# Attention with the PV product in three f32r passes instead of one fp32 pass, two steps behind the scores

## The chip, the cores and the metric

The kernel runs on one core of a Trainium2 chip. The metric is the device time of one execution in microseconds (us). TensorE (PE in the profile) multiplies matrices, VectorE (DVE), ScalarE (ACT) and GpSimd (POOL) work element by element, and SyncE (SP) issues DMAs. Each engine runs its own instructions in order; semaphores tie them together.

## The reference

One adaLN transformer block on x of shape 4 x 512 x 256: layer norm, attention with 16 heads of 128 whose weights are MXFP4 codes times block scales, a second layer norm, and a dense layer with eight routed LoRA experts. All of it is fp32. The change touches one product of the attention:

```python
q = _mxfp4_matmul(x, wq_codes, wq_scales) + bq      # k and v alike
scores = jnp.einsum('bqhd,bkhd->bhqk', q, k) / jnp.sqrt(jnp.float32(HEAD_DIM))
attn = jax.nn.softmax(scores, axis=-1)
out = jnp.einsum('bhqk,bkhd->bqhd', attn, v)        # "PV": 512 x 512 times 512 x 128, per batch and head
...
x = x + ga * attn_out
h = _layernorm(x) * (1 + cb) + sb
x = x + gb * ffn(h)                                  # dense + top-2 LoRA experts
```

## The kernel before

**Tiling.** Heads go two at a time: 8 pairs of heads (`pair(p)`), and in a pair 8 steps s = 0 to 7, one for each of 4 batches and 2 heads, so 64 steps n = 8p + s. Pairs 1 to 6 are a hardware loop (`Fori`), pairs 0 and 7 are written out, with the input transposes in the first and the preparation of the FFN weights in the last. All 512 x 512 scores of a step lie in four PSUM banks, `score_ps[0..3]`, one for each 128 queries.

**Three passes.** `three` (line 875) makes an fp32 product of two f32r matrices and their remainders: hi x hi, hi x lo, lo x hi, three matmuls. Q, K, V projections, scores and the output projection are made so. PV is not: `weighted` (line 934) multiplies fp32 `v` with fp32 transposed probabilities, four matmuls of 128 x 512, each of which the trace shows as two records.

**A step, by engine.** PE: scores of step n in four blocks; projections of q and k for step n+1 (`project`, banks `qv_ps`, `ky_ps`); output projection of the block before last (`out_project`, banks `y_ps` = `score_ps[2:4]`); V projection for n+1 (`project_v`); PV of step n-1 (`weighted`). DVE: four row maxima (`maximum`), reciprocals of the sums (`inverse`), the low parts of o, q and k (`o_low`, `q_low`, `k_low`), four 32 x 32 block transposes of the probabilities (`turn`), and two additions of the projected output to `yT` (`y_add`). ACT: four exponentials, then the high parts `q_high`, `k_high`, then `v_out` and `o_high`. POOL: multiplies the four blocks of probabilities by the reciprocals (line 364), then a share of the preparation of the next pair's weights: `product` (codes times scales) and `parts` (high and low part). SP: 16 DMAs that move the 32 x 32 blocks from `pB` to `pT32`, so that the transposition is whole. ACT also issues the loads of the next pair's weights, three DMAs at the end of each of the steps 0 to 3 (`load_weights`).

**What sets the order.** The order on each engine is that in which the code is written. `turned(par, kt)` is the view of `pT32` that PV reads, 16 runs of 32 numbers; `par` is the parity of the step, for which there are two `pB`, two `pT32` and two banks `o_ps`. `landed` is the semaphore value at which all 16 DMAs of a step have landed.

**The tail.** After the last step PE, DVE, POOL and ACT still make the last PV, two output projections, four batches of second layer norm (`attended`, `statistics`, `ffn_rows`), `ffn_input`, LoRA and dense products.

Of the kernel before, what the change touches and what calls it, by code (L numbers as in the profile page):

```python
# [5 lines left out]
def bass_adaln_mxfp4_attention_moe_lora_kernel(  # L6
# [64 lines left out]
    with ExitStack() as ctx:  # L71
# [26 lines left out]
        v = sb("v", [P, 2, QT, PW])  # L98
# [3 lines left out]
        pT32 = sb("pT32", [P, 2, G, QT, QT, 32])  # L102
        o_hi, o_lo = sb("o_hi", [P, S], f32r), sb("o_lo", [P, S], f32r)
# [58 lines left out]
        o_ps = [bank("o_even"), bank("o_odd")]  # L162
        y_ps = score_ps[2:4]
# [74 lines left out]
        def load_weights(queue, m, p):  # L238
# [57 lines left out]
        def _(pool):  # L296
# [44 lines left out]

            inverse_std(1)
# [16 lines left out]
            def pair(p, first=False, last=False):  # L359
                for s in range(SPP):  # L360
                    n = SPP * p + s
                    for i in range(QT):
                        pool.wait_ge(inv_ok, QT * n + i + 1)
                        pool.tensor_tensor(prob[:, i], prob[:, i], inv_sum[:, i:i + 1].to_broadcast([P, S]),  # L364
                                           ALU.mult).then_inc(prob_ok, 1)
                    if first and s in INPUT_AT:
                        inverse_std(INPUT_AT[s])
                    if s < 2:
                        if s == 0:
                            product("o", p)  # L370
                        if not first:
                            pool.wait_ge(y_mm, DC * (n - 1))
                        parts("o", p, s)
                    elif not last:
                        if s < 5:
                            product("vqk"[s - 2], p + 1)
                        elif s == 6:
                            pool.wait_ge(v_mm, n + 2)
                            parts("v", p + 1, 0)
                        else:  # L380
                            pool.wait_ge(k_mm, n + 2 if s == 5 else n + 1)
                            parts("q", p + 1, s // 6)
                            parts("k", p + 1, s // 6)
# [26 lines left out]
        def _(act):  # L410
# [37 lines left out]
            def v_out(count, par, half):  # L448
                act.wait_ge(v_mm, count)
                act.activation(v[:, par, 2 * half:2 * half + 2, :], qv_ps[:, :].rearrange("p (t f) -> p t f", t=2),  # L450
                               ACT.Copy).then_inc(v_ok, 1)

            def o_high(count, j):
                act.wait_ge(o_mm, count)
                act.activation(o_hi[:, :], o_ps[j][:, :], ACT.Identity, bias=bias_now[:, 2, j:j + 1]).then_inc(o_hi_ok, 1)  # L455
# [16 lines left out]
            def pair(p, first=False, last=False):  # L472
                for s in range(SPP):
# [3 lines left out]
                    if not early:  # L477
                        o_high(n - 1, s % 2)
                    if s == 1:
                        if not early:  # L480
                            act.wait_ge(o_hi_ok, n - 1)
                        act.activation(bias_now[:, 2], bias[:, 2, bass.ds(2 * p, 2)], ACT.Copy).then_inc(bias_ok, 1)
                        act.wait_ge(bias_ok, 2 * p + 2)
# [23 lines left out]
                    if end:  # L507
                        for i in range(2):
                            act.wait_ge(gbb_mm, i + 1)
                            act.activation(gb_row[:, 2 * i:2 * i + 2], (ky_ps, qv_ps)[i][:, :].rearrange("p (b d) -> p b d", b=2),  # L510
                                           ACT.Copy).then_inc(gbb_ok, 1)
                    if not end:
# [5 lines left out]
                    if not end:  # L518
                        v_out(n + 2, batch_of(s + 1) % 2, (s + 1) % 2)
# [57 lines left out]
            ffn_input_out(1)  # L577
            o_high(N, 1)
# [15 lines left out]
        def _(dve):  # L594
# [135 lines left out]
            def pair(p, first=False, last=False):  # L730
                for s in range(SPP):
# [25 lines left out]
                    if new:  # L757
                        dve.wait_ge(ld_x[new], 16)
                    maximum(0)
# [14 lines left out]
                    if not early:  # L774
                        o_low(n - 1, s % 2, head_slice(p, s - 2))
# [8 lines left out]
                    if not end:  # L784
                        q_low(n + 2, head_slice(p, s + 1))
                    turn(2)
                    if new:
                        normalise(new)
                    turn(3)
# [19 lines left out]

            attended(1)  # L810
            o_low(N - 1, 0, slice(FEAT // P - 2, FEAT // P - 1))
# [3 lines left out]
            ffn_rows(1)  # L815
            attended(2)
            o_low(N, 1, slice(FEAT // P - 1, FEAT // P))
            ffn_rows(2)
            for c in range(DC):
                y_add(DC * (N - 1) + c + 1, B - 1, c, False, (o_ps[0], y_ps[0])[c])  # L820
# [53 lines left out]
        def _(pe):  # L874
# [329 lines left out]
```

## Time and profile before

| | us |
|---|---|
| median of 3 runs | 883.76 |
| lowest, highest | 882.42, 885.69 |
| profiled execution | 881.12 |
| its span | 879.0 |
| PE busy in it | 823.7 (94%) |
| DVE, POOL, ACT busy | 617.1, 404.1, 381.8 |
| steps 2 to 63 | about 55 to 798 |

The span is what the instructions cover; 2.1 us lie around it. "Busy" counts instructions only, not waits. In the middle of the run one step takes 11.71 us and a pair 93.7 us. The timeline gives an instruction's start and its duration; one that follows another without a wait starts before the record of the first ends, so the cost of one in a row is the distance of starts.

### The profile page before, as it was taken

How to read it: one execution, taken by the hardware profiler on the slowest of the kernel's cores; microseconds unless marked ns; L12 is line 12 of the kernel's file. 1: busy time of each engine (PE TensorE's matmuls, PEld its weight loads, DVE VectorE, ACT ScalarE, POOL GpSimd, SP SyncE). 2: the span in 40 equal slices, each digit the busy share in tenths (PEclk: the TensorE clock that was granted, in tenths of full speed). 3: DMA queues.
4: the chain of work that ended last, by engine and by line, in shares of the span. 5: the costliest groups of instructions: out<-in, count | busy, mean ns of one | idle time of the engine just before them, and what ended most of it. 6: DMA issues, size and time to landing. Idle time of an engine off the chain costs nothing.

```text
span 879.0 us, 13011 instructions
## 1 busy us (share of the span) xinstructions
PE 823.7 (94%) x3548; PEld 607.9 (69%) x3548; DVE 617.1 (70%) x1268; ACT 381.8 (43%) x852; POOL 404.1 (46%) x439
## 2 busy tenths in 40 slices
PE   3969899999999999999999999999999999998758
PEld 2746677777777777777777777777777777665556
DVE  3767676776777777777767777777777775767563
ACT  2543544444444445544444444544444443442321
POOL 4433355444544555445544554445545552433230
PEclk9999899999999999999999999999999999999889
DMA  6143334443344334443444335533443353333002
GB/s 199 50 111 109 80 83 106 130 123 93 90 131 134 94 89 113 138 118 88 112 132 115 89 89 140 140 88 89 130 133 98 90 154 94 76 84 78 19 1 96
DMA packets 73808, 90.61 MB, mean 103 GB/s; under 512 B 19571, under 2 KB 40501, under 8 KB 73781
## 3 DMA queue, kind: packets, MB, share of 16 engines
q1 hardware_dynamic: 55988, 74.02, 32.9%
q10 hardware_dynamic: 17792, 16.26, 6.2%
q8 instruction: 13, 0.21, 0.1%
q14 instruction: 15, 0.11, 0.0%
HBM read 21.01 MB, written 2.10 MB: 26 GB/s over the span
## 4 chain that ended last, share of the span: by engine, by line
PE 74%; SPq 8%; issue 6%; DVE 5%; POOL 3%; DMA 2%; ACT 2%; POOLq 0%; ACTq 0%; DVEq 0%
PE o_odd L938 12%; PE o_even L938 11%; PE score L878 8%; PE score L880 8%; PE score L879 8%; SPq L281 7%; PE qv L878 5%; PE qv L880 5%; PE qv L879 5%; PE ky L878 3%; PE ky L879 3%; PE ky L880 3%; POOL prob L364 2%; DVE neg_max L741 2%; DMA pT<-pB 1%
## 5 line engine op out<-in xcount | busy, mean ns | idle before, releaser
L364 POOL TENSOR_TENSOR prob<-prob,inv_sum 128x512 f32<-128x512 f32 x256 | 258.5, 1041 | 385.2 <-DVE inv_sum L746 384.9
L741 DVE TENSOR_REDUCE neg_max<-score 128x1 f32<-128x512 f32 x256 | 176.0, 691 | 195.7 <-PE score L880 195.4
L488 ACT ACTIVATE prob<-score,neg_max 128x512 f32<-128x512 f32 x256 | 175.6, 688 | 59.4 <-DVE neg_max L741 59.2
L752 DVE STREAM_TRANSPOSE pB<-prob 128x512 f32<-128x512 f32 x256 | 179.7, 703 | 8.8 <-POOL prob L364 1.0
L878 PE MATMUL score<-k_hi,q_hi 128*128 128x512 f32 x256 | 124.7, 487 | 6.6 <-ACT hT_hi L431 6.4
L938 PE MATMUL o_even<-pT,v 128*128 128x512 f32 x256 | 115.5, 593 | 1.9 <-DMA pT<-pB 1.9
L938 PE MATMUL o_odd<-pT,v 128*128 128x512 f32 x256 | 115.6, 594 | 1.6 <-DMA pT<-pB 1.6
L880 PE MATMUL score<-k_hi,q_lo 128*128 128x512 f32 x256 | 101.4, 396 | 0.0
L879 PE MATMUL score<-k_lo,q_hi 128*128 128x512 f32 x256 | 100.5, 393 | 0.0
L450 ACT ACTIVATE v<-qv 128x512 f32<-128x512 f32 x64 | 38.2, 597 | 134.9 <-PE qv L880 134.9
L701 DVE TENSOR_TENSOR yT<-score,yT 128x512 f32<-128x512 f32 x121 | 77.2, 676 | 3.9 <-PE score L880 3.9
L938 PEld LDWEIGHTS o_odd<-pT,v 128*128 128x128 f32 x256 | 46.2, 190 | 48.6 <-issue 48.0
L938 PEld LDWEIGHTS o_even<-pT,v 128*128 128x128 f32 x256 | 46.2, 190 | 48.4 <-issue 46.4
L878 PE MATMUL qv<-wv_hi,hT_hi 128*128 128x256 f32 x256 | 73.1, 285 | 5.3 <-DVE q_lo L682 5.3
L879 PE MATMUL qv<-wv_lo,hT_hi 128*128 128x256 f32 x256 | 72.9, 285 | 0.0
L880 PE MATMUL qv<-wv_hi,hT_lo 128*128 128x256 f32 x256 | 72.9, 285 | 0.0
L878 PEld LDWEIGHTS score<-k_hi,q_hi 128*128 128x128 f32 x256 | 48.5, 189 | 29.5 <-issue 21.9
L455 ACT ACTIVATE o_hi<-o_even,bias_now 128x512 fp32r<-128x512 f32 x32 | 22.0, 687 | 99.2 <-PE o_even L938 99.2
L879 PEld LDWEIGHTS score<-k_lo,q_hi 128*128 128x128 f32 x256 | 48.7, 190 | 21.5 <-issue 13.2
L446 ACT ACTIVATE k_hi<-ky,bias_now 128x512 fp32r<-128x512 f32 x64 | 44.2, 690 | 42.7 <-PE ky L880 42.7
L455 ACT ACTIVATE o_hi<-o_odd,bias_now 128x512 fp32r<-128x512 f32 x32 | 22.0, 688 | 80.6 <-PE o_odd L938 80.6
L880 PEld LDWEIGHTS score<-k_hi,q_lo 128*128 128x128 f32 x256 | 48.5, 189 | 11.5
(205 smaller groups left out, 1471.6 us busy)
## 6 DMA issues: line engine op xcount, KB each, us to landing
pT<-pB SPq DMA_DIRECT2D x1024, 64.0 KB, 2.0
out_dram<-x_nat SPq DMA_DIRECT2D x8, 256.0 KB, 2.1
stage<-in_L_attn_wv_codes_dram ACTq DMA_DIRECT2D x7, 256.0 KB
stage<-in_L_attn_wv_scales_dram ACTq DMA_DIRECT2D x14, 128.0 KB
stage<-in_L_attn_wq_codes_dram ACTq DMA_DIRECT2D x7, 256.0 KB
stage<-in_L_attn_wq_scales_dram ACTq DMA_DIRECT2D x14, 128.0 KB
stage<-in_L_attn_wk_codes_dram ACTq DMA_DIRECT2D x7, 256.0 KB
stage<-in_L_attn_wk_scales_dram ACTq DMA_DIRECT2D x14, 128.0 KB
```

Source lines behind the costliest of these rows:

```text
L281: sp.dma_start(flat(pT32[32 * g:32 * (g + 1), par, a]), flat(pB[32 * a:32 * (a + 1), par, g])).then_inc(p_land[par], 16)
L364: pool.tensor_tensor(prob[:, i], prob[:, i], inv_sum[:, i:i + 1].to_broadcast([P, S]), ALU.mult).then_inc(prob_ok, 1)
L446: act.activation(k_hi[:, :], ky_ps[:, :], ACT.Identity, bias=bias_now[:, 1, j:j + 1]).then_inc(k_hi_ok, 1)
L455: act.activation(o_hi[:, :], o_ps[j][:, :], ACT.Identity, bias=bias_now[:, 2, j:j + 1]).then_inc(o_hi_ok, 1)
L488: act.activation(prob[:, i], score_ps[i][:, :], ACT.Exp, bias=neg_max[:, i:i + 1], accum_out=row_sum[:, i:i + 1]).then_inc(exp_ok, 1)
L701: dve.tensor_tensor(yT[:, c, tokens(b)], bank[:, :], yT[:, c, tokens(b)], ALU.add).then_inc(y_ok, 1)
L741: dve.tensor_reduce(neg_max[:, i:i + 1], score_ps[i][:, :], AX.X, ALU.max, negate=True).then_inc(max_ok, 1)
L752: dve.transpose(pB[:, s % 2, :, i].rearrange("p g k q -> p k g q"), prob[:, i].rearrange("p (k g q) -> p k g q", k=QT, g=G)).then_inc(pB_o ...
L878: pe.matmul(dst, a_hi, b_hi, start=first, stop=False)
L879: pe.matmul(dst, a_hi, b_lo, start=False, stop=False)
L880: return pe.matmul(dst, a_lo, b_hi, start=False, stop=last)
L938: ins = pe.matmul(o_ps[par][:, :], v[:, vpar, kt, j * HD:(j + 1) * HD], turned(par, kt), start=(kt == 0), stop=(kt == QT - 1))
```

## The change

PV is made with `three`: 12 matmuls of 128 x 512 a step. For that V and the probabilities need high and low parts.

- V: ACT copies the bank twice, to `v_hi` (f32r) and to `v32` (fp32); POOL subtracts (`v_low`). `v_out` moves from the end of a step to the start of the next one, ahead of the exponentials.
- Probabilities: ACT copies the four landed blocks to `pT_hi` (`prob_high`, after `k_high`, ahead of the weight loads); the low parts of blocks 0 and 1 are subtracted on DVE, those of blocks 2 and 3 on POOL (`prob_low`), at the start of their step, ahead of the maxima and of the multiplications.
- PV of step n-2 stands right behind the scores of step n. `o_high` moves behind the exponentials, `o_low` behind the second `turn`.
- One bank `o_ps[0]` takes PV; the other becomes the bank y of output column block 0.
- The high part of the V weights goes from POOL to ACT (step 7), their low part stands on POOL in step 7 behind `v_low`; products and parts of the other weights move by a step or so.
- In the tail, one more PV, with `prob_high` and `prob_low` for the last two steps.

GpSimd:

```diff
+            def v_low(count, par, half):
+                pool.wait_ge(v_hi_ok, count)
+                pool.wait_ge(v_ok, count)
+                pool.tensor_tensor(v_lo[:, par, 2 * half:2 * half + 2], v32[:, :, :],
+                                   v_hi[:, par, 2 * half:2 * half + 2].bitcast(f32), ALU.subtract).then_inc(v_lo_ok, 1)
+
+            def prob_low(n, par):
+                for kt in (2, 3):
+                    pool.wait_ge(p_hi_ok, QT * n + kt + 1)
+                    pool.tensor_tensor(split(pT_lo, kt), turned(par, kt), split(pT_hi, kt).bitcast(f32),
+                                       ALU.subtract).then_inc(p_lo_b, 1)
...
                     n = SPP * p + s
+                    if not (first and s < 2):
+                        prob_low(n - 2, s % 2)
                     for i in range(QT):
...
+                    if not (first and s == 0):
+                        v_low(n + 1, batch_of(s) % 2, s % 2)
...
+                        if s == 3:
+                            product("v", p + 1)
+                            product("q", p + 1)
+                        elif s == 4:
+                            product("k", p + 1)
+                        elif s > 5:
+                            if s == 7:
+                                pool.wait_ge(w_hi_ok["v"], p + 2)
+                                pool.tensor_tensor(w_lo["v"][:, :, :], w32["v"][:, :, :], w_hi["v"][:, :, :].bitcast(f32),
+                                                   ALU.subtract).then_inc(w_ok["v"], 1)
+                            pool.wait_ge(k_mm, n + 1)
+                            parts("q", p + 1, s - 6)
+                            parts("k", p + 1, s - 6)
```

ScalarE:

```diff
+            def prob_high(par, have):
+                act.wait_ge(p_land[par], have)
+                for kt in range(QT):
+                    act.activation(split(pT_hi, kt), turned(par, kt), ACT.Copy).then_inc(p_hi_ok, 1)
...
+                    if not start:
+                        v_out(n + 1, batch_of(s) % 2, s % 2)
...
-                    if not end:
-                        v_out(n + 2, batch_of(s + 1) % 2, (s + 1) % 2)
+                    if not start:
+                        prob_high((s - 1) % 2, landed(p, s - 1))
```

VectorE:

```diff
+            def prob_low(n, par):
+                for kt in (0, 1):
+                    dve.wait_ge(p_hi_ok, QT * n + kt + 1)
+                    dve.tensor_tensor(split(pT_lo, kt), turned(par, kt), split(pT_hi, kt).bitcast(f32),
+                                      ALU.subtract).then_inc(p_lo_a, 1)
...
+                    if not early:
+                        prob_low(n - 2, s % 2)
                     maximum(0)
                     maximum(1)
```

TensorE, `weighted` and the tail:

```diff
-            def weighted(vpar, j, par, have):
-
-                pe.wait_ge(p_land[par], have)
+            def weighted(n, vpar, j):
+
                 for kt in range(QT):
-                    ins = pe.matmul(o_ps[par][:, :], v[:, vpar, kt, j * HD:(j + 1) * HD], turned(par, kt),
-                                    start=(kt == 0), stop=(kt == QT - 1))
+                    pe.wait_ge((p_lo_a, p_lo_b)[kt // 2], 2 * n + kt % 2 + 1)
+                    cut = (slice(None), vpar, kt, slice(j * HD, (j + 1) * HD))
+                    ins = three(o_ps[0][:, :], (v_hi[cut], v_lo[cut]), (pT_hi[:, kt], pT_lo[:, kt]), kt == 0, kt == QT - 1)
...
             ffn_input(1)
+            weighted(N - 1, (B - 1) % 2, 1)
             pe.wait_ge(y_ok, DC * (N - 1))
             rows_of_y(2)
-            weighted((B - 1) % 2, 1, 1, landed(PAIRS - 1, SPP - 1))
```

**VectorE, one step in the last pair.** The names are output<-inputs; `neg_max` is the maxima, `pB` the block transposes, `yT` the additions. Before, from the maxima on:

```order
L741 TENSOR_REDUCE neg_max<-score 128x1 x3
L746 RECIPROCAL inv_sum<-row_sum 128x1
L741 TENSOR_REDUCE neg_max<-score 128x1
L746 RECIPROCAL inv_sum<-row_sum 128x1
L692 SCALAR_TENSOR_TENSOR o_lo<-o_even,vecT,o_hi 128x512
L746 RECIPROCAL inv_sum<-row_sum 128x1
```

And after:

```order
L752 TENSOR_TENSOR yT<-score,yT 128x512
L743 TENSOR_TENSOR pT_lo<-pT,pT_hi 128x512 x2
L792 TENSOR_REDUCE neg_max<-score 128x1 x3
L797 RECIPROCAL inv_sum<-row_sum 128x1
L792 TENSOR_REDUCE neg_max<-score 128x1
L797 RECIPROCAL inv_sum<-row_sum 128x1 x2
L803 STREAM_TRANSPOSE pB<-prob 128x4x4x32
L797 RECIPROCAL inv_sum<-row_sum 128x1
L803 STREAM_TRANSPOSE pB<-prob 128x4x4x32
L737 SCALAR_TENSOR_TENSOR o_lo<-o,vecT,o_hi 128x512
```

Two subtractions with both inputs in SBUF stand between the last addition and the first maximum, and `o_lo` stands two transposes later.

**GpSimd, steps 6 and 7 of a pair** (here of pair 0). `prob` is the multiplication by the reciprocals, `wv`, `wq`, `wk` the weights. Before:

```order
L364 TENSOR_TENSOR prob<-prob,inv_sum 128x512 x4
L332 TENSOR_TENSOR wv_hi<-stage,ones 128x512
L334 TENSOR_TENSOR wv_lo<-stage,wv_hi 128x512
L364 TENSOR_TENSOR prob<-prob,inv_sum 128x512 x4
L332 TENSOR_TENSOR wq_hi<-stage,ones 128x2x128
L334 TENSOR_TENSOR wq_lo<-stage,wq_hi 128x2x128
L332 TENSOR_TENSOR wk_hi<-stage,ones 128x2x128
L334 TENSOR_TENSOR wk_lo<-stage,wk_hi 128x2x128
```

And step 7 after:

```order
L359 TENSOR_TENSOR pT_lo<-pT,pT_hi 128x512 x2
L387 TENSOR_TENSOR prob<-prob,inv_sum 128x512 x4
L353 TENSOR_TENSOR v_lo<-v,v_hi 128x512
L408 TENSOR_TENSOR wv_lo<-stage,wv_hi 128x512
L340 TENSOR_TENSOR wq_hi<-stage,ones 128x2x128
L342 TENSOR_TENSOR wq_lo<-stage,wq_hi 128x2x128
L340 TENSOR_TENSOR wk_hi<-stage,ones 128x2x128
L342 TENSOR_TENSOR wk_lo<-stage,wk_hi 128x2x128
```

Three subtractions are new in every step, and the low part of the V weights has come from step 6 to step 7, the step whose V projection needs it.

## Rows read from the trace of the kernel before

**Rows 1.** The page: span, and busy time of each engine.

```profile
span 879.0 us, 13011 instructions
PE 823.7 (94%) x3548; PEld 607.9 (69%) x3548; DVE 617.1 (70%) x1268; ACT 381.8 (43%) x852; POOL 404.1 (46%) x439
```

**Rows 2.** One pair: stretch, length; busy PE, PEld, DVE, ACT, POOL; PE clock; DMA.

```profile
356.00:450.00 94.00, 94.00 (x402) 68.90 (x401) 69.81 (x139) 44.34 (x101) 47.51 (x50) 1.00 0.43 111
```

**Rows 3.** Chain of work: start, cost on the path, engine, output, line.

```profile
407.78 0.12 PE qv L880
...
408.62 3.44 PE o_odd L938 x8
412.05 0.23 PE score L878
```

**Rows 4.** Timeline, VectorE, one step: start, duration, line, operation [idle before].

```profile
412.78 2.08 DVE L741 TENSOR_REDUCE neg_max<-score 128x1 f32<-128x512 f32 x3 [2.88 <-PE score L880]
414.78 0.15 DVE L746 RECIPROCAL inv_sum<-row_sum 128x1 f32<-128x1 f32 x1
...
417.72 0.71 DVE L682 SCALAR_TENSOR_TENSOR q_lo<-qv,vecT,q_hi 128x512 fp32r<-128x512 f32 x1
418.35 1.44 DVE L752 STREAM_TRANSPOSE pB<-prob 128x512 f32<-128x512 f32 x2
419.72 0.71 DVE L687 SCALAR_TENSOR_TENSOR k_lo<-ky,vecT,k_hi 128x512 fp32r<-128x512 f32 x1
420.35 1.28 DVE L701 TENSOR_TENSOR yT<-score,yT 128x512 f32<-128x512 f32 x2
424.50 2.08 DVE L741 TENSOR_REDUCE neg_max<-score 128x1 f32<-128x512 f32 x3 [2.88 <-PE score L880]
```

**Rows 5.** Timeline, ScalarE, the same step.

```profile
413.51 0.69 ACT L488 ACTIVATE prob<-score,neg_max 128x512 f32<-128x512 f32 x1 [0.67 <-DVE neg_max L741]
...
420.37 0.60 ACT L450 ACTIVATE v<-qv 128x512 f32<-128x512 f32 x1 [2.10 <-PE qv L880]
```

**Rows 6.** Timeline, GpSimd, this step and the one before.

```profile
409.82 1.27 POOL L334 TENSOR_TENSOR wv_lo<-stage,wv_hi 128x512 fp32r<-128x512 f32 x1
415.01 4.03 POOL L364 TENSOR_TENSOR prob<-prob,inv_sum 128x512 f32<-128x512 f32 x4 [3.93 <-DVE inv_sum L746]
...
421.09 0.73 POOL L334 TENSOR_TENSOR wk_lo<-stage,wk_hi 128x256 fp32r<-128x256 f32 x1
```

**Rows 7.** Timeline: VectorE subtractions without and with GpSimd at work.

```profile
16.56 1.29 DVE L640 TENSOR_TENSOR hT_lo<-hT,hT_hi 128x512 fp32r<-128x512 f32 x2
...
38.30 1.70 DVE L640 TENSOR_TENSOR hT_lo<-hT,hT_hi 128x512 fp32r<-128x512 f32 x2
...
38.32 1.12 POOL L332 TENSOR_TENSOR wo_hi<-stage,ones 128x256 fp32r<-128x256 f32 x1
39.52 1.07 POOL L334 TENSOR_TENSOR wo_lo<-stage,wo_hi 128x256 fp32r<-128x256 f32 x1
```

**Rows 8.** SP's waits from 75 to 780 us (total, times, longest), and its DMAs.

```profile
SPq L281 <- DVE pB L752: 100.2, 59, 5.5
...
pT<-pB SPq DMA_DIRECT2D x1024, 64.0 KB, 2.0
```

**Rows 9.** Timeline, ScalarE's queue: the weight loads at a step's end.

```profile
361.78 0.39 ACTq L249 DMA_DIRECT2D stage<-in_L_attn_wk_codes_dram  x1
362.27 1.20 ACTq L253 DMA_DIRECT2D stage<-in_L_attn_wk_scales_dram  x2
```

**Rows 10.** Timeline, PE: the first PV and the scores behind it.

```profile
50.71 3.67 PE L938 MATMUL o_even<-pT,v 128*128 128x512 f32 x8 [1.66 <-DMA pT<-pB]
...
55.01 0.48 PE L878 MATMUL score<-k_hi,q_hi 128*128 128x512 f32 x1
```

**Rows 11.** Timeline, the tail: ScalarE and VectorE.

```profile
824.27 1.44 ACT L554 ACTIVATE pB<-score,modT 128x512 f32<-128x512 f32 x2 [0.33 <-PE score L1093]
825.15 1.29 DVE L720 TENSOR_TENSOR x_nat<-score,x_nat 128x512 f32<-128x512 f32 x2 [1.63 <-PE score L964]
```

More of the change, by code:

```diff
@@ L102, in bass_adaln_mxfp4_attention_moe_lora_kernel @@
         pT32 = sb("pT32", [P, 2, G, QT, QT, 32])
+        pT_hi = sb("pT_hi", [P, QT, S], f32r)
+        pT_lo = sb("pT_lo", [P, QT, S], f32r)
         o_hi, o_lo = sb("o_hi", [P, S], f32r), sb("o_lo", [P, S], f32r)
@@ L391, in _ @@
             N = SPP * PAIRS
+            prob_low(N - 2, 0)
             gate(2)
@@ L394, in _ @@
             inverse_std(B + 1)
+            prob_low(N - 1, 1)
             times_gb(0)
@@ L476, in pair @@
                     early = first and s < 2
[L477 to L483, printed above, removed]
+                    if not start:
+                        v_out(n + 1, batch_of(s) % 2, s % 2)
+                    if s == SPP - 1 and not last:
+                        act.wait_ge(w_prod["v"], p + 2)
+                        act.activation(w_hi["v"][:, :, :], w32["v"][:, :, :], ACT.Copy).then_inc(w_hi_ok["v"], 1)
                     for i in range(QT):
@@ L577, in _ @@
             ffn_input_out(1)
+            prob_high(1, landed(PAIRS - 1, SPP - 1))
             o_high(N, 1)
@@ L783, in pair @@
                     turn(1)
-                    if not end:
-                        q_low(n + 2, head_slice(p, s + 1))
+                    if not early:
+                        o_low(n - 1, head_slice(p, s - 2))
                     turn(2)
@@ L788, in pair @@
                         normalise(new)
+                    if not end:
+                        q_low(n + 2, head_slice(p, s + 1))
                     turn(3)
@@ L808, in _ @@
             N = SPP * PAIRS
+            prob_low(N - 2, 0)
             attended(1)
-            o_low(N - 1, 0, slice(FEAT // P - 2, FEAT // P - 1))
+            o_low(N - 1, slice(FEAT // P - 2, FEAT // P - 1))
             ffn_rows(0)
@@ L1009, in pair @@
                             pe.wait_ge(exp_ok, QT * (n - 1) + i + 1)
-                        if i >= 2 and not (first and s < 3):
-                            pe.wait_ge(y_ok, DC * (n - 3) + i - 1)
+                        if i == 3 and not (first and s < 3):
+                            pe.wait_ge(y_ok, DC * (n - 2))
                         if i >= 2 and first and s - 1 in INPUT_AT:
@@ L1016, in pair @@
                               True, True).then_inc(s_mm, 1)
+                    if not early:
+                        pe.wait_ge(v_lo_ok, n - s % 2)
+                        if first and s == 2:
+                            pe.wait_ge(h_hi, DC * 2)
+                        if not (first and s < 3):
+                            pe.wait_ge(o_ok, n - 2)
+                        if end:
+                            pe.wait_ge(gbb_ok, 2)
+                        weighted(n - 2, batch_of(s - 2) % 2, s % 2)
                     if end:
-                        pe.wait_ge(gbb_ok, 2)
+                        pe.wait_ge(v_ok, n + 1)
                         rows_of_y(0)
@@ L1050, in pair @@
                         project_v(batch_of(nxt), nxt % 2).then_inc(v_mm, 1)
-                    if not start:
-                        pe.wait_ge(v_ok, n + s % 2)
-                        if first and s == 1:
-                            pe.wait_ge(h_hi, DC * 2)
-                        if not (first and s < 3):
-                            pe.wait_ge(o_ok, n - 2)
-                        weighted(batch_of(s - 1) % 2, (s - 1) % 2, (s - 1) % 2, landed(p, s - 1))
                     if first and s in INPUT_AT:
```

77 lines of the change are left out of this document (42 added, 35 removed).

## The prediction

> **What bounds the kernel now.** The page first [rows 1]: PE is busy 823.7 of 879.0 us, DVE 617.1, POOL 404.1, ACT 381.8. A pair in the middle [rows 2]: PE is busy all of its 94 us at full clock (1.00, the 2.4 GHz level), DVE 69.8, POOL 47.5, ACT 44.3. So in the loop PE sets the time, and a step is what its matmuls cost on the path [rows 3]: 0.227 us for 512 columns in one f32r pass, 0.12 for 256, 3.44 for PV. 12 (scores) + 12 (q, k) + 6 (output) passes are 6.81, twelve half ones (V) 1.43, PV 3.44: 11.68. DVE's first maxima are 11.72 apart [rows 4], which agrees.
>
> **PE: what is removed.** 12 passes x 0.227 = 2.73 replace 3.44: 0.71 less, so 11.0 us a step, 88 a pair for 93.7. Over 61 steps that is 43 us, if PE stays the bound.
>
> **The next bounds.** *SP.* It waits 100.2 us in 705 [rows 8], so 16 issues take (705 - 100) / 60 steps = 10.05 us, and a transfer lands 2.0 us after its issue. A block turned at X is in `pT32` at X + 12.2. Throughput holds (10.05 < 11.0), latency is long.
>
> *DVE.* From the first maximum to the end of the second addition it takes 8.8 us (412.78 to 421.6) [rows 4]. `o_low` no longer fills the time until the first product comes from POOL (0.23 after the reciprocal starts, then 1.04 [rows 4, 6]), which adds 0.6. So 9.4: three maxima 2.0, from there to the fourth transpose's end 5.5, `k_low` and additions 1.9. To this comes D, the time of the two subtractions. Free of others two cost 0.60 each (1.29 recorded for two [rows 7]): D = 1.2, step 10.6, hidden under PE's 11.0.
>
> *POOL.* A subtraction of two 128x512 SBUF inputs costs 1.27, the four multiplications 4.03, the four parts of a q/k slice 2.75 [rows 6]. New per step are two subtractions (2.54) and `v_low` (1.27): 4.03 + 3.81 = 7.85 without weights, 10.6 in step 6, 11.9 in step 7, about 77.5 us a pair.
>
> *ACT.* New: four copies of landed blocks. No row shows a copy from SBUF in such runs; V's copy from PSUM is 0.60 long, and exponentials, 0.69 long with their read, stand 0.69 apart [rows 5]. I take 0.55 each, between 0.5 and 0.7. The second copy of V adds 0.5. In steps 0 to 3 the loads' three DMA issues (0.39 + 1.20, with gaps 1.7 [rows 9]) now stand between `prob_high` and the next step's `v_out`, thus ahead of the exponentials. They were hidden by an idle ACT. The ring over two steps is X + 12.2 (landing) + 2.2 (copies) + 1.0 (V) + 0.8 (exponential) + 5.5 (to the next X of that parity) = 21.7, 10.85 a step; with the loads 23.4, 11.7 a step. So even undisturbed, four of eight steps get little of the 0.71.
>
> **Where the gain goes: two engines at one port.** [Rows 7] is what decides. Two DVE subtractions with both inputs in SBUF took 1.29 while POOL stood still, and 1.70 while it worked; POOL's two operations in that place took 1.12 and 1.07, for 0.61 and 0.72 otherwise. They excluded each other: DVE's first ran, POOL's began behind it (0.5 late), DVE's second behind POOL's (0.4 late). In the loop before no DVE operation has two SBUF inputs; the change puts two into every step, and every POOL operation there reads SBUF.
>
> *By the rule of the Trainium skill* ("SBUF — State Buffer", Who interferes with whom) a DVE operation with two SBUF inputs and a GpSimd operation that reads SBUF exclude each other for the whole instruction. The trace agrees (0.4 and 0.5 us). Without that rule the sum would be the rival "no collision" below.
>
> When do they meet? Take DVE's last addition as zero and T as the step. The previous X is at -1.9, the one that counts at -1.9 - T; landing is at 10.3 - T, and POOL's first `prob_low` (third copy done, +1.75) can start at 12.05 - T. With T = 11.0 that is 1.05, after DVE's second subtraction started (0.6): no meeting. With T of 11.5 or more it is before 0.6: then POOL's 1.27 goes between DVE's two, D = 0.6 + 1.27 + 0.6 = 2.5, and T = 9.4 + 2.5 = 11.9, which keeps them meeting. If POOL comes first as well, D is 3.7 and T 13.1. T is pushed over 11.5 by the loads on ACT (11.7), by the two products of step 3, which end 0.4 us after DVE wants the port, and by steps 6 and 7. I take T = 11.9, D's lower value: at 12.05 - 11.9 = 0.15 DVE is just first.
>
> **A pair.** Step 7: POOL's multiplications start 2.0 + 0.23 behind D, about 5.9 us after PE's scores; + 4.03 + 1.3 (`v_low`) + 1.3 (low part of the V weights) = 12.5, when PE's V projection may start; it wanted to at 10.5. So about 14.2. The stall lets DVE catch up: steps 0 and 1 about 11.0 and 11.2. Steps 2 to 6 take 11.9, and 0.7 more once, for step 3's second product. Sum 11.0 + 11.2 + 59.5 + 0.7 + 14.2 = 96.6, for 93.7: +2.9.
>
> **The ends.** Start: step 1 loses its PV; scores that began at 55.01 can begin when the inputs are transposed, about 51.7: -3.3 [rows 10]. Tail: PV of block 63 now needs `prob_high`, which stands on ACT behind `ffn_input_out(1)` (ends 825.7 [rows 11]), then POOL's two subtractions. With 2.0 us of lag from DVE's longer sequence: 827.7 + 1.75 + 2.54 + last block 0.7 + row transposes 0.9 = 833.7, for 825.15 when `attended(2)` starts now [rows 11]. PE made those rows ahead of PV before and makes them behind it after. What follows is a chain of DVE and POOL: +8.6.
>
> **The sum** against the profiled 881.1: start -3.3; pair 0 from step 3: +3.5; six pairs x 2.9 = +17.4; pair 7, seven steps without weight work: 0 (11.0 + 11.2 + 59.5 = 81.7 for 82.0); tail +8.6. 881.1 + 26.2 = 907.3. The median before stands 0.3% over the profiled time; I say 908.
>
> **Rivals.**
> *No collision, PE bound (faster).* If DVE's second subtraction goes ahead of a waiting POOL, D stays near 1.2 and T is the larger of 11.0 and the ring, whose slack in steps 5 to 8 pays some of the loads. Pair: 88 + 2 (loads) + 1.5 (V weights, step 7) = 91.5, -2.2 each. 881 - 3.3 - 7.5 x 2.2 + 8.6 = 870; without the loads' cost 860. It holds as long as POOL's first `prob_low` comes later than 0.6 after DVE's first. For it: in light steps that is so. Against it: [rows 7], and steps 3, 6, 7, where POOL is still at work. If PE were the bound in every step and the tail free: 840, which needs every cover to hold.
>
> *The gain is just eaten.* T about 11.5 between the two regimes, a pair 93.5: 881 - 3.3 + 8.6 = 886, or 881 if the tail's lag is half.
>
> *Worse.* POOL first at the port often (D 3.1 on average, T 12.5), or POOL slower on runs of 32 numbers, which no row shows: +3 a pair more, 930. PE's clock could fall to 1.2 GHz behind the stall of step 7; each such time costs up to 2 us: 920.
>
> *The change doesn't do what it says.* The order above shows the 12 passes in one row behind the scores, so that PV itself is shorter I take as given.
>
> **How the numbers follow.** Collision kept up (895 to 922): 0.52; worse (over 922): 0.12; gain just eaten (878 to 895): 0.16; no collision (under 878): 0.20. The range takes the first, the third and most of the fourth, from 866 to 924: about 0.8. Faster by over 0.5% (under 879.3): 0.21; within 0.5%, about what a measurement of this kernel can tell from no change: 0.08; slower: 0.71.
>
> **What would show it.** Right: PV on PE 2.73 us long; PE no longer all busy in the loop, waiting for `p_lo`, `o_lo` or `q_lo`; steps of 11.9 and one of 14 a pair; DVE's `pT_lo` subtractions with a mean near 1.2 us instead of 0.69, and POOL's `pT_lo` over 1.3; `attended(2)` some 8 us later after the last scores than now. Wrong: DVE's subtractions at 0.69, steps of 11.0 to 11.4 and PE busy all the time. A mean of POOL's `pT_lo` far over 1.3 without DVE at work would be the worse case. If the steps after 0 to 3 alone are long and ACT never waits there, the loads are the cause and not the port.

## The result, and the profile of the changed kernel

The changed kernel takes 911.03 us (median of 4 runs, 906.94 to 915.88), the kernel before 883.09: ratio 1.033 with a 95% interval of 1.030 to 1.036. The profiled execution took 906.94 us, its span is 905.0. Forecast was 908.

The page of the changed kernel, to be held against [rows 1]:

```profile
span 905.0 us, 14369 instructions
PE 808.7 (89%) x3804; PEld 651.5 (72%) x3804; DVE 773.5 (85%) x1396; ACT 545.4 (60%) x1179; POOL 672.1 (74%) x624
```

PE is busy 15 us less and waits more. DVE is busy 156 us more, POOL 268, ACT 164. One pair in the loop (columns as in [rows 2]):

```profile
434.50:530.70 96.20, 92.02 (x433) 73.45 (x432) 89.69 (x153) 64.50 (x141) 81.28 (x74) 1.00 0.42 109
```

PE, busy all the time in [rows 2], now stands idle 4.2 us of each pair at full clock; DVE is busy 89.7 of 96.2 us, for 69.8 of 94. Where the 26 us of the span come from, read from the first maxima of the steps on DVE:

| stretch | before | changed | difference |
|---|---|---|---|
| start, from the span's start to step 8 | 141.0 | 148.9 | +7.9 |
| six pairs of the loop | 565.3 | 574.2 | +8.9 |
| last pair, step 56 to 63 | 92.7 | 90.0 | -2.7 |
| from step 63 to the end | 80.0 | 92.0 | +12.0 |

Between the first maxima of step 0 and step 8 alone the start takes 111.4 before and 119.6 changed, 8.3 more; step 0 comes 0.4 earlier in the changed kernel. (The expectation of e5_start below gives 7.9 for this stretch; 7.9 is the figure from the span's start.)

The first pair of the loop takes 93.3, the five others 96.2 each (before 95.8, then 93.7 to 94.3).

One step on DVE, the change's answer to [rows 4]:

```profile
397.13 3.20 DVE L743 TENSOR_TENSOR pT_lo<-pT,pT_hi 128x512 fp32r<-128x512 f32 x2
400.26 1.27 DVE L792 TENSOR_REDUCE neg_max<-score 128x1 f32<-128x512 f32 x2
...
408.71 0.68 DVE L752 TENSOR_TENSOR yT<-score,yT 128x512 f32<-128x512 f32 x1
409.31 2.82 DVE L743 TENSOR_TENSOR pT_lo<-pT,pT_hi 128x512 fp32r<-128x512 f32 x2
412.05 1.87 DVE L792 TENSOR_REDUCE neg_max<-score 128x1 f32<-128x512 f32 x3
```

and the same stretch on POOL:

```profile
396.78 3.00 POOL L359 TENSOR_TENSOR pT_lo<-pT,pT_hi 128x512 fp32r<-128x512 f32 x2
...
408.59 2.98 POOL L359 TENSOR_TENSOR pT_lo<-pT,pT_hi 128x512 fp32r<-128x512 f32 x2 [1.02 <-ACT pT_hi L494]
414.07 4.04 POOL L387 TENSOR_TENSOR prob<-prob,inv_sum 128x512 f32<-128x512 f32 x4 [2.49 <-DVE inv_sum L797]
```

DVE's two subtractions hold it 3.13 us (397.13 to 400.26), for 1.2 when it has the port alone. POOL begins 0.35 and 0.7 us ahead of DVE and is itself stretched from 2.5 to 3.0; two subtractions of each, one after the other, are 2 x 1.27 + 2 x 0.6 = 3.7 us, and together they end 3.5 us after POOL's start. Taken one by one, the four show that the engines take turns:

```profile
396.78 1.29 POOL L359 TENSOR_TENSOR pT_lo<-pT,pT_hi 128x512 fp32r<-128x512 f32 x1
397.13 1.49 DVE L743 TENSOR_TENSOR pT_lo<-pT,pT_hi 128x512 fp32r<-128x512 f32 x1
398.04 1.75 POOL L359 TENSOR_TENSOR pT_lo<-pT,pT_hi 128x512 fp32r<-128x512 f32 x1
398.55 1.78 DVE L743 TENSOR_TENSOR pT_lo<-pT,pT_hi 128x512 fp32r<-128x512 f32 x1
```

POOL's first ends at 398.1, DVE's first 0.5 later, POOL's second 1.2 after that, DVE's second 0.5 later again. After that POOL idles 2.5 us, waiting for DVE's reciprocal: the meeting delays the work that both then wait for. The rest of DVE's row, 400.26 to 409.31, is 9.05.

### The profile page after: what moved, and what is told of

Same layout as the page of the kernel before. It is cut to its first block, busy times and chain, and to the rows that moved or that the text cites. A ratio compares the mean times of both kernels' runs of the same rounds, so it can differ in the third digit from the quotient of the medians.

```text
span 905.0 us, 14369 instructions
## 1 busy us (share of the span) xinstructions
PE 808.7 (89%) x3804; PEld 651.5 (72%) x3804; DVE 773.5 (85%) x1396; ACT 545.4 (60%) x1179; POOL 672.1 (74%) x624
## 4 chain that ended last, share of the span: by engine, by line
DVE 36%; issue 17%; POOL 16%; PE 14%; ACT 9%; SPq 6%; DMA 2%; DVEq 0%; ACTq 0%; POOLq 0%
DVE pT_lo L743 10%; DVE pB L803 8%; POOL prob L387 8%; ACT prob L525 5%; SPq L289 4%; DVE neg_max L792 4%; DVE yT L752 4%; DVE k_lo L732 3%; POOL pT_lo L359 3%; DVE o_lo L737 2%; DVE q_lo L727 2%; POOL v_lo L353 2%; DVE z L679 2%; PE qv L933 1%; PE o L933 1%
## 5 line engine op out<-in xcount | busy, mean ns | idle before, releaser
L359 POOL TENSOR_TENSOR pT_lo<-pT,pT_hi 128x512 fp32r<-128x512 f32 x128 | 189.1, 1499 | 39.8 <-ACT pT_hi L494 39.6
L494 ACT ACTIVATE pT_hi<-pT 128x512 fp32r<-128x512 f32 x256 | 140.4, 620 | 57.3 <-DMA pT<-pB 57.3
L792 DVE TENSOR_REDUCE neg_max<-score 128x1 f32<-128x512 f32 x256 | 164.6, 676 | 11.3 <-PE score L935 11.2
L743 DVE TENSOR_TENSOR pT_lo<-pT,pT_hi 128x512 fp32r<-128x512 f32 x128 | 164.9, 1327 | 3.9 <-ACT pT_hi L494 3.9
L933 PE MATMUL o<-pT_hi,v_hi 128*128 128x512 f32 x256 | 106.6, 417 | 15.0 <-DVE pT_lo L743 10.4
L934 PE MATMUL o<-pT_lo,v_hi 128*128 128x512 f32 x256 | 101.4, 396 | 0.0
L935 PE MATMUL o<-pT_hi,v_lo 128*128 128x512 f32 x256 | 101.4, 396 | 0.0
L933 PE MATMUL qv<-wv_hi,hT_hi 128*128 128x256 f32 x256 | 74.5, 291 | 25.6 <-DVE q_lo L727 15.3
L353 POOL TENSOR_TENSOR v_lo<-v,v_hi 128x512 fp32r<-128x512 f32 x64 | 83.0, 1297 | 4.8 <-ACT v L485 4.8
L933 PEld LDWEIGHTS o<-pT_hi,v_hi 128*128 128x128 f32 x256 | 48.9, 191 | 44.0 <-DVE pT_lo L743 22.6
L933 PEld LDWEIGHTS qv<-wv_hi,hT_hi 128*128 128x128 f32 x256 | 49.8, 194 | 32.1 <-DVE q_lo L727 16.4
L489 ACT ACTIVATE o_hi<-o,bias_now 128x512 fp32r<-128x512 f32 x64 | 44.6, 697 | 29.9 <-PE o L935 29.7
```

The lines of the kernel that those rows point to most:

```text
L353: pool.tensor_tensor(v_lo[:, par, 2 * half:2 * half + 2], v32[:, :, :], v_hi[:, par, 2 * half:2 * half + 2].bitcast(f32), ALU.subtract).th ...
L359: pool.tensor_tensor(split(pT_lo, kt), turned(par, kt), split(pT_hi, kt).bitcast(f32), ALU.subtract).then_inc(p_lo_b, 1)
L489: act.activation(o_hi[:, :], o_ps[0][:, :], ACT.Identity, bias=bias_now[:, 2, j:j + 1]).then_inc(o_hi_ok, 1)
L494: act.activation(split(pT_hi, kt), turned(par, kt), ACT.Copy).then_inc(p_hi_ok, 1)
L743: dve.tensor_tensor(split(pT_lo, kt), turned(par, kt), split(pT_hi, kt).bitcast(f32), ALU.subtract).then_inc(p_lo_a, 1)
L792: dve.tensor_reduce(neg_max[:, i:i + 1], score_ps[i][:, :], AX.X, ALU.max, negate=True).then_inc(max_ok, 1)
```

## The experiments

All edits are to the changed kernel, or to one of its variants, as said. What a variant is compared with is its span and its steps; where a median of several runs is given, its ratio to the kernel before has a 95% interval. Theory: the two engines exclude each other at the port, which makes D, the time of DVE's two subtractions, long. Rivals: DVE's added work as such; POOL's; the copies and loads on ACT. In the cuts of code below, `...` stands for what is left out.

**POOL waits until DVE's two low parts of the step are done** (e1_gate):

```
 def prob_low(n, par):          # POOL
+    pool.wait_ge(p_lo_a, 2 * n + 2)
     for kt in (2, 3):
```

> One wait is added to the changed kernel: GpSimd begins its two subtractions of a step (prob_low) only when VectorE has finished its two of the same step. Nothing else moves and no work is saved. Port theory: the two engines exclude each other at SBUF, and most of the loss is that GpSimd's 1.27 us subtractions get in front of and between VectorE's two. With the wait VectorE's two take 1.3 us together for 3.0 in the profile of the changed kernel, the step is then VectorE's 9.1 + 1.2 = 10.3, so PE's 11.0 decides; the loop pair goes from 96.2 us to 90 to 92, and the whole from 911 to about 875. Rival, too much work of their own on VectorE or GpSimd: the wait starts GpSimd's work later by 0.6 us and saves nothing, so 911 to 920 and a pair of 96 or more.

870.63 us (4 runs), ratio 0.986 [0.983, 0.989]: one wait more makes a kernel that loses 3.3% into one that gains 1.4%. The gain is clear of the noise, though under 2%. The low parts in the loop, first of the changed kernel, then of this one (count, then busy us and mean ns of one):

```profile
L743 DVE TENSOR_TENSOR pT_lo<-pT,pT_hi 128x512 fp32r<-128x512 f32 x80 | 110.7, 1422 | 0.0
...
L359 POOL TENSOR_TENSOR pT_lo<-pT,pT_hi 128x512 fp32r<-128x512 f32 x80 | 119.7, 1519 | 5.8 <-ACT pT_hi L494 5.6
```

```profile
L744 DVE TENSOR_TENSOR pT_lo<-pT,pT_hi 128x512 fp32r<-128x512 f32 x32 | 24.1, 795 | 0.0
```

and one pair of this kernel:

```profile
416.86:507.09 90.23, 88.76 (x433) 74.31 (x432) 79.68 (x153) 65.34 (x141) 77.62 (x74) 1.00 0.45 116
```

PE is the bound again (88.8 of 90.2), with light steps at 10.9, as the prediction's PE row of 11.0 has it. DVE's time falls by 10 us a pair for the same instructions. The tail, though, is longer still, 96.9 for 92.0, at a granted clock of 0.84 for 0.89 over it. POOL's wait can't be the whole reason, since the tail of e3_small_pool below, which has no such wait, takes 96.3 at the same 0.84. PE's longest waits in the tails of the changed kernel and e1_gate are the same (5.6 us for DVE's `pT_lo`, 2.8 to 2.9 for `gb_row`); what makes the rest longer is open.

**All four low parts on DVE** (e2_all_dve), so that the two never meet there:

```
 def prob_low(n, par):          # POOL
+    return
 def prob_low(n, par):          # DVE
-    for kt in (0, 1):
+    for kt in range(QT):
...
 pe.wait_ge(o_ok, N - 2)        # PE, tail
+pe.wait_ge(v_lo_ok, N)
```

The added wait on PE keeps PV of step 62 behind `v_low`, which POOL's low parts did before.

> All four low parts of the probabilities on VectorE, none on GpSimd. Port theory: a subtraction costs 0.6 us by itself, so VectorE's four take 2.4 plus one wait of up to 0.7 where GpSimd is at its weight work; step 9.1 + 2.5 = 11.6 to 11.9, pair 93 to 95, the whole 890 to 905. Rival, VectorE's subtractions are long by themselves (1.33 us in the mean of the profile, from runs of 32 numbers): four take 5.3, step 14.4, the whole over 1050.

901.68 us (4 runs), ratio 1.022 [1.019, 1.025]; pairs 94.5, steps of 11.46 in the main. Four subtractions hold DVE 0.6 each (774 ns recorded, two at a time overlapping), 2.4 us a step: 9.05 + 2.4 = 11.45. DVE doing everything is better than DVE sharing with POOL, by 1.7 us a pair; against the kernel before, the loss of 2.2% is too near 2% to call it clearly slower.

**POOL's low parts cut to 32 of 512 columns** (e3_small_pool), and **DVE's cut likewise** (e4_small_dve); the rest of these low parts is set to zero once at the start, so that the product leaves them out:

```
-  tensor_tensor(split(pT_lo, kt), turned(par, kt), split(pT_hi, kt)...)
+  tensor_tensor(split(pT_lo, kt)[:, 0, 0], turned(par, kt)[:, 0, 0], split(pT_hi, kt)[:, 0, 0]...)
```

> GpSimd's two subtractions of a step are left in place but cut to 32 of 512 columns (the rest of these low parts stays zero), so nothing of GpSimd stands in VectorE's way for long. Port theory: VectorE's two take 1.3 us, pair about 90 to 91, the whole about 870. Rival, VectorE has too much work of its own: VectorE does the same work as before, so the pair stays near 96 and the whole near 905.

> VectorE's two subtractions of a step are cut to 32 of 512 columns (the rest of these low parts stays zero), GpSimd's stay whole. Port theory: GpSimd's run at 1.27 us each (1.50 in the mean before), VectorE's step is 9.1 + 0.3, PE decides, pair about 90 to 91, the whole about 870. Rival, GpSimd has too much work of its own: GpSimd does the same work as before, so the pair stays near 96 and the whole near 905. Read with the kernel in which GpSimd's are cut: if both fall to about the same time, neither engine's own load but their meeting is the cause.

858.13 and 863.37 us (one run each); from the second pair of the loop on, pairs take 88.6 to 88.9 and 88.5. Both totals lie under the 870 expected. With POOL's short, DVE's full-size ones are back at 773 ns; with DVE's short, POOL's are at 1292, for 1519 in the changed kernel:

```profile
L745 DVE TENSOR_TENSOR pT_lo<-pT,pT_hi 128x512 fp32r<-128x512 f32 x49 | 36.0, 773 | 0.0
```

```profile
L359 POOL TENSOR_TENSOR pT_lo<-pT,pT_hi 128x512 fp32r<-128x512 f32 x50 | 63.6, 1292 | 23.6 <-ACT pT_hi L494 23.6
```

Neither engine's load by itself is the cause: taking either away gives back all of the loop's loss, with the other's left whole. ACT has its copies and loads in both, at 11.1 a step on the mean. In e1_gate both loads are whole, and only the meeting of the low parts is gone: it is the meeting.

**One meeting in place of two** (e9_gate_one): the wait of e1_gate for `2 * n + 1`, DVE's first low part only.

> The kernel with POOL's wait, but POOL waits for the first of DVE's two low parts of a step only, so that one pair of instructions meets instead of two (changed kernel) or none (e1_gate). Theory of the port (in the changed kernel two low parts of DVE take 3.0 us in place of 1.3 because DVE stands one whole POOL subtraction, some 1.27, for each that it meets less what both had already run): the first takes 0.65 to 0.7, the second 1.3 or some more, D about 2.0, DVE's row 9.05 + 2.0 = 11.05, just PE's 10.9, and POOL starts 0.6 us earlier, which the steps 7 and 0, bound by POOL's row, get back: pair 90 to 91.5, 868 to 878 in all. Rival (a throughput that the two engines share, so that what matters is the sum of their work in the stretch and not who meets whom): the first is stretched too, D about 2.6, DVE's row 11.6, pair 93, 885 to 890.

866.44 us (one run), pairs 89.2: the first theory's side, but 1.6 us under its 868 to 878, and shorter than with the full wait. So not by its arithmetic. I had put DVE's second at 1.3; DVE's mean is as in e3_small_pool, and it is POOL that pays:

```profile
L744 DVE TENSOR_TENSOR pT_lo<-pT,pT_hi 128x512 fp32r<-128x512 f32 x48 | 35.1, 773 | 0.0
```

```profile
L360 POOL TENSOR_TENSOR pT_lo<-pT,pT_hi 128x512 fp32r<-128x512 f32 x48 | 68.1, 1440 | 25.8 <-DVE pT_lo L744 20.5 <-ACT pT_hi L495 5.3
```

A step of it on DVE, then on POOL:

```profile
455.47 1.65 DVE L744 TENSOR_TENSOR pT_lo<-pT,pT_hi 128x512 fp32r<-128x512 f32 x2
```

```profile
456.60 1.67 POOL L360 TENSOR_TENSOR pT_lo<-pT,pT_hi 128x512 fp32r<-128x512 f32 x1 [0.63 <-DVE pT_lo L744]
```

DVE's first stands behind POOL's instruction before it (to 455.97) and ends near 456.5. POOL, released by it, gets going at 456.60, when DVE's second has just begun; that ends at 457.1 undisturbed, and POOL's first takes 1.67: 0.4 of waiting and 1.27. So the price of this meeting falls on POOL, which came second, and POOL is still through earlier than with the full wait. Of the 1.0 us by which the pair is shorter, 0.3 is PE's wait for `wv_lo` (1.1 for 1.4); the rest lies in gaps too short for the list of waits, and is not placed.

**The start** (e5_start), on e1_gate:

```
+    if not end:
+        q_low(n + 2, head_slice(p, s + 1))
     if new:
         normalise(new)
-    if not end:
-        q_low(n + 2, head_slice(p, s + 1))
```

> The kernel with POOL's wait (e1_gate, 870.6), and in the two early steps that take in a new batch DVE makes the low part of q ahead of the normalisation of the new rows instead of behind it. Theory: the start's loss (7.9 us from the first maxima of step 0 to those of step 8) comes from that order, because PE's projection of v waits 14.7 us in 3 there for q_lo (5.3 in the kernel before), and the normalisation runs 3.1 and 4.2 us ahead of q_lo. Then those two steps get 2.5 to 3.5 us shorter each, since the transposes of the normalised rows stay behind z and only the 2.7 us of the v projection moves forward: 864 to 866, step 8 at 139 to 140. Rival: the start's loss is the two half-clock stretches and the wait for hT_hi (6.1 us in 4, as before); then 870 to 871 and step 8 stays at 144.9.

865.47 us (one run). PE's waits in the start, before, in the changed kernel, and here (total, times, longest):

```profile
PE qv L878 <- DVE q_lo L682: 5.3, 3, 2.2
```

```profile
PE qv L933 <- DVE q_lo L727: 15.3, 3, 6.7
```

```profile
PE qv L934 <- DVE q_lo L728: 6.5, 2, 3.8
...
PE score L955 <- DVE yT L753: 4.6, 1, 4.6
```

Step 8 comes at 141.6 for 144.9: 3.2 us, not the 5 to 6 expected, since in the second of the two steps a wait of 4.6 for the additions to `yT`, which now stand behind the normalisation, takes the place of the wait for `q_lo`. In the changed kernel the normalisation ahead of `q_lo` took 3.09 us, for 2.14 in the kernel before:

```profile
48.71 3.09 DVE L679 TENSOR_SCALAR z<-x_nat,mv,rstd 128x256 f32<-128x256 f32 x4 [0.92 <-POOL rstd L321]
51.72 0.74 DVE L727 SCALAR_TENSOR_TENSOR q_lo<-qv,vecT,q_hi 128x512 fp32r<-128x512 f32 x1
```

How good is one number of this kind? Up to step 7 the starts of e1_gate, e6_wv and e7_tail are the same code, and step 7 comes at 133.2, 134.4 and 131.2; e5_start, e8_all and e11_all_tail2 have `q_low` ahead, and there it comes at 130.0, 128.6 and 130.0. So some 3 us for this order is seen in three pairs of traces, and a single start is good to about 3 us.

The rest of the start's +7.9 is not placed. e1_gate brings step 8 from 148.9 to 144.9 and e3_small_pool to 143.4, but e2_all_dve (150.6) and e4_small_dve (148.2), where DVE's and POOL's low parts don't meet either, or hardly, do not; so that it is the port is not shown. The granted clock is a part of it too: 0.89 from step 0 to step 8, for 0.94 in the kernel before.

**`wv_lo` ahead of `v_low` in step 7** (e6_wv), on e1_gate.

> The kernel with POOL's wait, and in step 7 of a pair POOL makes the low part of wv ahead of the low part of v instead of behind it. Theory: PE's wait of 1.4 us for wv_lo (once a pair, 7 pairs) shrinks by the 1.25 us of v_lo to some 0.2, and the pair goes from 90.2 to 89.1: 862 to 863.5 in all. Rival: the next wait takes its place (v_lo of the step, which PV of the next step needs, or DVE's own row, 11.0 of the step's 11.7): the pair stays within 0.3 of 90.2, 868.5 to 870.6.

870.08 us (one run), pairs 90.3 for 90.2: the rival. Step 7 gets 0.3 us shorter, step 0 0.3 longer. Why is seen on POOL, here in e6_wv from step 7 on:

```profile
503.82 1.30 POOL L353 TENSOR_TENSOR v_lo<-v,v_hi 128x512 fp32r<-128x512 f32 x1
505.07 0.62 POOL L340 TENSOR_TENSOR wq_hi<-stage,ones 128x256 fp32r<-128x256 f32 x1
...
507.99 0.74 POOL L342 TENSOR_TENSOR wk_lo<-stage,wk_hi 128x256 fp32r<-128x256 f32 x1
508.69 2.54 POOL L360 TENSOR_TENSOR pT_lo<-pT,pT_hi 128x512 fp32r<-128x512 f32 x2
511.18 4.04 POOL L388 TENSOR_TENSOR prob<-prob,inv_sum 128x512 f32<-128x512 f32 x4
```

POOL works without a break from step 7 into step 0. Its row is the bound there, and what is done first only chooses who waits: PE for `wv_lo` (1.4 once a pair in e1_gate), or PE for POOL's `pT_lo` and DVE for the first product.

**The tail** (e7_tail on e1_gate; e10_tail_no_gate, the same edits on the changed kernel itself):

```
 # ACT: the two copies of gb_row ahead of step 63's exponentials
 o_high(N - 1, 0)
+prob_high(1, landed(PAIRS - 1, SPP - 1))
 ffn_input_out(0)
+o_high(N, 1)
 lora_out(0)
 ffn_input_out(1)
-prob_high(1, landed(PAIRS - 1, SPP - 1))
-o_high(N, 1)
 # DVE: prob_low(N-2) ahead of attended(0); prob_low(N-1) behind ffn_rows(0)
 # PE
+weighted(N - 1, (B - 1) % 2, 1)
 lora_rows(0)
 ffn_input(1)
-weighted(N - 1, (B - 1) % 2, 1)
```

> The kernel with POOL's wait, and in step 63 and behind it the low parts of the last two steps as soon as their inputs are there: the two copies of gb_row ahead of the exponentials of step 63, DVE's low parts of step 62 ahead of the first attended rows, the high and low parts of step 63 right behind the output of step 61's successor, PE's last PV ahead of the low-rank rows of batch 0. Theory: the tail's loss (80.1 us from the first maxima of step 63 to the end before, 96.9 with POOL's wait) is the two PV that stand in the tail behind the FFN's work: waits of 2.8 for gb_row, 3.3 and 2.3 for DVE's low parts, and PV of step 63 at 807.5 where its inputs could be there at 801; the tail gets 8 to 11 us shorter: 860 to 863. Rival: the tail is bound by the chain of normalisations (z waits, 13.5 us in 4) that only moves with the last x1 rows, or by the half clock: 867 or more.

> The changed kernel without POOL's wait, and with the edits of e7_tail alone. With POOL's wait the tail from the first maxima of step 63 went from 96.9 to 84.5 us. Theory (the tail's loss is where the low parts of the last two steps stand in the queues, not the port): from 91.95 to 81 to 84, the loop pairs stay at 96.2, 896 to 899 in all. Rival (in the tail the loss is that DVE and POOL meet): the tail stays over 88 and the whole over 903.

859.39 and 899.48 us (one run each), 0.6 and 0.5 us outside the ranges given. The tail goes from 96.9 to 84.5 with POOL's wait, and from 92.0 to 84.0 without, where the loop pairs stay at 96.2. So of the tail's 12.0 us the places in the queues carry 8, with no help from POOL's wait; the other 4 stay, and no run takes them apart. The changed kernel's tail, PE then DVE, with the last PV and the rows that answer to [rows 11]:

```profile
845.16 0.50 PE L933 MATMUL o<-pT_hi,v_hi 128*128 128x512 f32 x1 [2.34 <-DVE pT_lo L743]
848.15 0.50 PE L933 MATMUL o<-pT_hi,v_hi 128*128 128x512 f32 x1 [0.27 <-POOL pT_lo L359]
848.95 1.03 PE L1019 MATMUL score<-ident,yT 128*128 128x128 f32 x8
```

```profile
844.41 1.29 DVE L743 TENSOR_TENSOR pT_lo<-pT,pT_hi 128x512 fp32r<-128x512 f32 x2 [2.75 <-ACT pT_hi L494]
...
849.58 1.29 DVE L771 TENSOR_TENSOR x_nat<-score,x_nat 128x512 f32<-128x512 f32 x2 [3.88 <-PE score L1019]
```

In e7_tail the same rows of `x_nat` are at 802.23, 29.2 us after step 63's first maximum, for 36.5 in the changed kernel.

**Together** (e8_all: e5, e6 and e7; e11_all_tail2: with batch 3's last rows ahead of batch 2's FFN work; e12_best: that with e9's wait).

> The three edits of e5_start, e6_wv and e7_tail together on the kernel with POOL's wait. If the losses in the start, in step 7 and in the tail are separate, their gains add: 870.6 less about 5, 7.5 and 9, so 848 to 852, ratio to the kernel before 0.960 to 0.966. If they share one bound (PE's own rows in the loop, 10.9 a step), less: 856 to 860.

> e8_all (855.8), and in the tail the last rows of batch 3 go ahead of the FFN work of batch 2: PE's output projection of step 63 and rows_of_y(3) before ffn_input(2) and the low-rank rows of batch 2, the matching order on ACT and DVE (yT first, then z of batch 2). In e8_all z of batch 3 lands at about 821 in a tail whose last 31 us (from its transposes to the end) PE works through alone, so each us by which z comes earlier is one off the time, less what the half clock takes: expected 3 to 5 us, 851 to 853. Rival: attended(3) only waits elsewhere (for gated rows or for POOL's rstd), and the tail keeps its 83.7 us: 855 to 857.

> e11_all_tail2 (851.6) with POOL waiting for the first of DVE's two low parts only, as in e9_gate_one. There the pair was 89.2 us against 90.2 with the full wait (one look). If that 1.0 us a pair is PE's own row getting shorter waits on POOL in steps 7 and 0, it adds to the other edits: 851.6 less 7 to 8, so 843 to 846, ratio 0.955 to 0.960. If the two share it (the wv_lo moved ahead of v_lo makes PV of step 0 wait for POOL), less: 848 to 851.

855.78 us, ratio 0.971 [0.969, 0.974] (4 runs); 851.56, 0.964 [0.959, 0.968] (4); 845.34, 0.958 [0.955, 0.961] (6). e8_all missed its 848 to 852 and came out at the edge of its rival's 856 to 860, since I had counted the 7.5 us of `wv_lo` that e6_wv did not give and 5 for a start that gave 3 to 5; e11's tail is 79.4 for 83.7, as expected. The last one is 4.2% under the kernel before and 7.2% under the changed kernel, with a loop that PE bounds:

```profile
411.44:500.52 89.08, 88.59 (x433) 74.32 (x432) 79.79 (x153) 65.19 (x140) 80.15 (x74) 1.00 0.45 118
```

## Why the prediction was right, point by point

*PE's row*: 11.0 a step forecast; 10.9 where nothing disturbs it (e1_gate). Right.

*The port*: right as mechanism in the loop, and shown by e1, e3 and e4 from three sides. By the Trainium skill ("SBUF — State Buffer", Who interferes with whom) the two kinds of instruction exclude each other for their whole length; the trace agrees, 3.5 us for what is 3.7 one after the other. The rival without a collision, 870, is what e1_gate takes (870.6), but that is luck too: its pair was put at 91.5 and takes 90.2, while its start (-3.3) measured +3.9 and its tail (+8.6) +16.8.

*D and the chain*: here two terms were wrong against each other. I took D = 2.5, DVE just first at 0.15. POOL is 0.35 to 0.7 ahead, so D is 2.7 to 3.2. And the rest of DVE's row is 9.05, not 9.4: the three maxima hold it 1.8, not 2.0, from there to the fourth transpose's end it is 5.4, not 5.5, and `k_low` with the additions 1.8, not 1.9. Steps 1 to 5 come at 11.75 to 12.23, 12.05 on the mean, for 11.9; so D is 3.0 on the mean there. The step that failed is "at 12.05 - 11.9 = 0.15 DVE is just first". Its 12.2 from the turn to the landing holds from the fourth transpose's start (12.2 to 12.6 to ACT's first copy), but the sum counts it from that transpose's end at -1.9, and from there it is 11.5 to 11.9. With 11.5 the same line gives -0.55, POOL first, as measured. D then isn't the 3.7 named for that case, since DVE comes 0.35 to 0.7 later and waits only for what is left of POOL's first.

*The pair*: 96.2, forecast 96.6, but spread otherwise. Step 7 has no stall of 14.2; PE waits 1.5 there for `wv_lo` (7.3 in 5), for 2.0 forecast. The long interval is the next one, 13.5 from step 0's first maximum to step 1's, since POOL carries its row over, and DVE waits 1.55 for the first product:

```profile
439.16 0.71 DVE L803 STREAM_TRANSPOSE pB<-prob 128x512 f32<-128x512 f32 x1 [1.55 <-POOL prob L387]
```

I took steps 0 and 1 at 11.0 and 11.2; they are 13.5 and 12.15, and steps 6 and 7 10.9 and 11.5. (14.2 wasn't the sum of its own terms either: 11.9 and a wait of 2.0 are 13.9.) That the sum is right owes something to luck: I had POOL's load right and put its price one step early.

*Six pairs*: +17.4 forecast, +8.9 measured, though a pair was only 0.4 off. Two reasons: before's pairs average 94.2, not the 93.7 I subtracted from (some steps of [rows 4]'s kind take 12.36), 0.5 a pair; and the first pair of the loop runs at 93.3. In it steps of 10.25 and 10.68 stand, behind one of 12.97, and DVE gets the port alone:

```profile
206.43 1.28 DVE L743 TENSOR_TENSOR pT_lo<-pT,pT_hi 128x512 fp32r<-128x512 f32 x2
```

Both are under PE's own 10.9, so they catch up on the long step and are no state that could last. From the second pair on, steps 1 to 5 of every pair stay at 11.75 to 12.23: "which keeps them meeting" holds for the loop once it is there.

*ACT's loads*: forecast to put 1.7 into the ring of two steps, 11.7 a step, in the four steps that have them. Wrong. With POOL's wait steps 1 and 2, which have loads, take 10.98 and 10.9, like those without. The issues run beside the `prob_high` copies, as at the end of step 1 in e1_gate:

```profile
49.90 0.63 ACT L495 ACTIVATE pT_hi<-pT 128x512 fp32r<-128x512 f32 x1 [3.12 <-DMA pT<-pB]
49.91 0.38 ACTq L253 DMA_DIRECT2D stage<-in_L_attn_wq_codes_dram  x1
50.33 0.56 ACTq L257 DMA_DIRECT2D stage<-in_L_attn_wq_scales_dram  x1
50.44 1.13 ACT L495 ACTIVATE pT_hi<-pT 128x512 fp32r<-128x512 f32 x2
```

The copy itself, 0.55 by the estimate, is 0.53 to 0.55. In the forecast the loads were what pushed T over 11.5, in part. The steps collide without them: in light steps as in loaded ones.

*The start*: -3.3 and +3.5 forecast, +7.9 measured. PV gone from step 1 gave nothing, because PE waited there for `q_lo` anyway. The order that shows this stood in the change: `q_low` moved behind `normalise(new)`, which takes 3.1 us beside POOL. I had not priced it. It is worth 3 us by e5_start; the rest is open, as said there.

*The last pair*: 0 forecast, 81.7 for 82.0, and -2.7 measured, 90.0 for 92.7. The forecast took steps of the loop for it, but it has the FFN's preparation in it, with steps up to 15.3 before and 15.8 changed. Why it gains 2.7 no run shows.

*The tail*: +8.6 forecast, +12.0 measured. The chain named (`prob_high` behind `ffn_input_out(1)`, then POOL) is what the rows show: `x_nat` starts 36.5 us after step 63's first maximum for 26.2 before, 10.3 later. What I had missed is PV of step 62, which now stands in the tail too and waits 3.3 us for DVE's low parts behind the rows of batch 0.

In all: +26.2 forecast, +26.1 measured in the span; start 7.7 too low, loop 8.5 too high, last pair 2.7 too high, tail 3.4 too low. The mechanism and the pair were right, and the nearness of the total is the luck of four errors that cancel.

## What to carry to other kernels

Before a VectorE instruction with two SBUF inputs is shared out to GpSimd "in parallel", look whether the two halves start together: if they do, one semaphore that lets VectorE go first can be worth more than the split (911 to 871 us here), and here it did better still when it covered all but VectorE's last instruction (866 in one run). When work moves one step later in a software pipeline, list every instruction that it pushes back in the prologue and the drain: here the start and the tail lost 20 us together, of which two orders in the queues were found to hold 3 and 8, while the loop, which the change was about, lost 9. If reordering on one engine moves a wait without shrinking it, as in e6_wv, look whether that engine works there without a break: then its queue is the bound, not the order.

## What was not expected of the hardware

- Who waits at the port is decided by who is running, instruction by instruction. With both engines queued, they take turns, one instruction each (3.13 us for DVE's two in place of 1.2); a POOL subtraction that arrives when DVE's has just begun is the one stretched, 1.67 for 1.3, and DVE's median stays at 684 ns.
- The meeting keeps itself up: from the second pair of the loop to its last, steps 1 to 4 come at 12.0 to 12.2 us with DVE's two at 2.9 to 3.1, though without it the same row of DVE would take 10.3 (9.05 + 1.2) and PE's 10.9.
- DMA issues on ACT's queue (0.38 + 0.56 + 0.56) cost the activations beside them next to nothing: the four copies in that place take 2.2 us with or without them.
